# Two tiles' adapter rows in one turn, and 64-row products in pairs on the two halves of the array

## What is computed

```python
def _L1_cond_ref(x, adapter_mapping, W, b, lora_As, lora_Bs):
    base_out = jnp.einsum('bti,oi->bto', x, W) + b
    A = lora_As[adapter_mapping]
    Bm = lora_Bs[adapter_mapping]
    lora_h = jnp.einsum('bti,bir->btr', x, A)
    lora_out = jnp.einsum('btr,bro->bto', lora_h, Bm)
    return base_out + lora_out * SCALING
...
x = x + _L1_ffn_ref(_L1_cond_ref(x, itok_B_0_23, ...), ...)
```

## Time and profile before

| | |
|---|---|
| median of three runs | 466.69 us |
| the profiled execution | 466.59 us, span of its core 464.7 us |
| mean granted TensorE clock | 0.996 of full speed |
| TensorE matmuls | 2758, busy 447.0 us |
| VectorE, ScalarE, GpSimd busy | 306.9, 151.0, 72.6 us |
| a batch in the middle | about 38 us |

### The profile page before, as it was taken

How to read it: one execution, slowest core, us unless ns; L and a number is a source line. 1 busy time by engine, 2 the same in 40 slices (tenths; PEclk the granted TensorE clock), 3 DMA queues, 4 the chain that set the end, 5 groups by cost and what they waited for, 6 DMA issues and landing times.

```text
span 464.7 us, 7813 instructions
## 1 busy us (share of the span) xinstructions
PE 447.0 (96%) x2758; PEld 414.9 (89%) x2758; DVE 306.9 (66%) x911; ACT 151.0 (32%) x314; POOL 72.6 (16%) x62
## 2 busy tenths in 40 slices
PE   4988799999999999999999999999999999999997
PEld 4977799999988898889999999999999999999986
DVE  3897637574758688578557648738747755864852
ACT  4685212322222463234233224224323423321310
POOL 2040000000002412402402222120240230220110
PEclk9999899999999999999999999999999999999999
DMA  8993131111001101104103201211210310300302
GB/s 253 383 413 138 45 149 45 47 46 44 20 35 45 50 23 49 46 18 143 48 6 107 69 28 63 98 46 62 98 45 17 135 57 1 109 9 1 107 2 90
DMA packets 15151, 37.08 MB, mean 80 GB/s; under 512 B 2439, under 2 KB 7305, under 8 KB 15118
## 3 DMA queue, kind: packets, MB, share of 16 engines
q1 hardware_dynamic: 15022, 36.66, 22.7%
q0 software_dynamic: 96, 0.00, 0.2%
HBM read 27.07 MB, written 9.59 MB: 79 GB/s over the span
## 4 chain that ended last, share of the span: by engine, by line
PE 83%; DVE 12%; ACT 2%; issue 2%; DMA 1%; SPq 0%; DVEq 0%; ACTq 0%
PE banks L1239 25%; PE banks L1241 25%; PE banks L1240 25%; PE banks L1246 4%; DVE G L789 2%; DVE WbTlo L789 2%; PE banks L1471 2%; PE banks L1283 1%; DVE left L789 1%; DMA ws_lo_raw<-in_W_dram 1%; DVE ws_lo L789 1%; PE banks L1380 0%; DVE x_raw L973 0%; DVE G_raw L1086 0%; DVE w0s_lo L789 0%
## 5 line engine op out<-in xcount | busy, mean ns | idle before, releaser
L1239 PE MATMUL banks<-G,left 128*128 128x460 f32 x224 | 88.0, 393 | 0.0
L1240 PE MATMUL banks<-G,left 128*128 128x460 f32 x224 | 82.9, 370 | 0.0
L1241 PE MATMUL banks<-G,left 128*128 128x460 f32 x224 | 82.9, 370 | 0.0
L1239 PE MATMUL banks<-WbThi,ws_hi 128*128 128x460 f32 (+1 forms) x216 | 74.6, 345 | 4.3 <-DVE WbTlo L789 3.8
L474 POOL TENSOR_TENSOR xTlo<-x_raw,xThi 128x512 fp32r<-128x512 f32 x28 | 37.9, 1374 | 238.5 <-ACT xThi L572 114.6
L1241 PE MATMUL banks<-WbThi,ws_lo 128*128 128x460 f32 (+1 forms) x216 | 73.4, 340 | 0.0
L1240 PE MATMUL banks<-WbTlo,ws_hi 128*128 128x460 f32 (+1 forms) x216 | 73.1, 338 | 0.0
L526 ACT ACTIVATE left<-x_raw 128x512 fp32r<-128x512 f32 x64 | 38.7, 627 | 59.9 <-DVE x_raw L946 29.3
L1239 PEld LDWEIGHTS banks<-WbThi,ws_hi 128*128 128x128 f32 x216 | 40.6, 188 | 8.8 <-DVE WbTlo L789 4.9
L1239 PEld LDWEIGHTS banks<-G,left 128*128 128x128 f32 x224 | 42.4, 189 | 4.5 <-DVE wzTlo L789 0.3
L1241 PEld LDWEIGHTS banks<-G,left 128*128 128x128 f32 x224 | 42.1, 188 | 4.7
(11 more groups left out here) (178 smaller groups left out, 938.2 us busy)
## 6 DMA issues: line engine op xcount, KB each, us to landing
x_raw<-in_xT_dram SPq DMA_DIRECT2D x16, 512.0 KB, 3.8
out_dram<-ybuf SPq DMA_DIRECT2D x14, 512.0 KB, 2.7
x_raw<-in_W_dram SPq DMA_DIRECT2D x8, 512.0 KB, 3.3
WbTlo_raw<-in_F_dram SPq DMA_DIRECT2D x4, 920.0 KB, 12.8
w0s_lo_raw<-in_W_dram SPq DMA_DIRECT2D x6, 512.0 KB, 9.4
Fbuf<-fe_hi_dram SPq DMA_DIRECT2D x16, 64.0 KB
WbTlo_raw<-in_F_dram SPq DMA_DIRECT2D x1, 960.0 KB, 6.6
out_dram<-ybuf SPq DMA_DIRECT2D x3, 230.0 KB, 2.4
```

Of the source, the lines that this page charges most:

```text
L1239: pe.matmul(out_, l[0], r[0], start=start, stop=False, **kw)
L1240: pe.matmul(out_, l[0], r[1], start=False, stop=False, **kw)
L1241: return pe.matmul(out_, l[1], r[0], start=False, stop=stop, **kw)
```

## The change

`hs` becomes 128 columns wide: each tile gets one half of 64, with the three copies of h and the ones packed at 0, 17 and 34. One turn per batch (`turn_hs`, without arguments) transposes both, and one copy of ScalarE fills the one `hsT` of 128 rows, tile 0 in rows 0 to 63 and tile 1 in rows 64 to 127. `Ebuf` and `Fbuf` hold the slot's rows twice, once in each half, so SyncE issues six loads each instead of three. `adapter` and the new `adapters` issue one matmul of 64 rows for each tile, one right after the other, on the two halves; their results go to different PSUM banks. The F products leave `lora` and stand in pairs: the first two parts after `lora(0, 1)`, the third after `lora(1, 2)`. The turn and the E products take the places of the second tile's. The turn of `wz` of the first tile moves from step 22 to 24 in the batches that have a next one. `y_c12` waits for the last pair. The diff, cut to its core:

```diff
--- before.py
+++ after.py
+    HP = P // 2
...
-        Ebuf = sb("Ebuf", [96, RC], F32R)
+        Ebuf = sb("Ebuf", [P, RC], F32R)
...
-        hs = sb("hs", [P, 96], F32R)
+        hs = sb("hs", [P, P], F32R)
...
-        hsT = [sb(f"hsT{i}", [96, P], F32R) for i in range(2)]
+        hsT = sb("hsT", [P, P], F32R)
...
-        Fbuf = sb("Fbuf", [96, D], F32R)
+        Fbuf = sb("Fbuf", [P, D], F32R)
...
+        def hs_of(half):
+
+            return hs[:, half * HP:half * HP + 2 * (R + 1)], hs[:, half * HP + 2 * (R + 1):half * HP + 3 * R + 2]
+
+        def hs_rows(t, half):
+            return t[half * HP:(half + 1) * HP]
...
-            blocks = [(0, fe_hi_dram), (32, fe_lo_dram), (64, fe_hi_dram)]
+            blocks = [(half * HP + at, src) for half in range(2)
+                      for at, src in ((0, fe_hi_dram), (R + 1, fe_lo_dram), (2 * (R + 1), fe_hi_dram))]
+            bias_rows = [blocks[i] for i in (0, 1, 3, 4)]
 
             def load_e(b):
                 for p, src in blocks:
...
-            sp.wait_ge(memsets_done, 2)
+            sp.wait_ge(memsets_done, 1)
             load_e(0)
-            for p, src in blocks[0:2]:
+            for p, src in bias_rows:
                 sp.dma_start(Ebuf[p + R:p + R + 1, :].bitcast(F32), src[P:P + 1, 0:RC]).then_inc(e_in, 16)
...
-            sp.wait_ge(memsets_done, 3)
+            sp.wait_ge(memsets_done, 2)
             load_fb(0)
-            for p, src in blocks[0:2]:
+            for p, src in bias_rows:
                 sp.dma_start(Fbuf[p + R:p + R + 1, :].bitcast(F32), src[P:P + 1, RC:MC]).then_inc(f_in, 16)
...
-            def hsT_part(t, half):
-                wait_earlier(act, lora_done, t * 3 - 3 if not isinstance(t, int) or t > 1 else 0)
-                hi_half(ths_done, t + 1, hsT[half][:, :], pt_h1[0:96, :], hsT_ready)
+            def hsT_part(b):
+                wait_earlier(act, lora_done, b * 6)
+                hi_half(ths_done, b + 1, hsT[:, :], pt_h1, hsT_ready)
...
                 s_part(b, turn, 2)
-                hsT_part(m, 0)
-                hsT_part(m + 1, 1)
+                hsT_part(b)
...
-            dve.memset(hs[:, R:R + 1].bitcast(F32), 1.0).then_inc(memsets_done, 1)
-            dve.memset(hs[:, 32 + R:32 + R + 1].bitcast(F32), 1.0).then_inc(bias_step, 1)
+            for half in range(2):
+                for i in range(2):
+                    at = half * HP + i * (R + 1) + R
+                    ins = dve.memset(hs[:, at:at + 1].bitcast(F32), 1.0)
+            ins.then_inc(bias_step, 1)
...
             def y_c12(b):
                 dve.wait_ge(p_done, b * 7 + 7)
+                dve.wait_ge(lora_done, b * 6 + (6 if b < NB - 1 else 5))
...
             def hs_part(t, half):
 
                 dve.wait_ge(h1_done, t + 1)
-                wait_earlier(dve, ths_done, t)
-                dve.tensor_copy(hs[:, 0:64].rearrange("p (b c) -> p b c", b=2)[:, :, 0:R],
+                wait_earlier(dve, ths_done, t // 2)
+                twice, rest = hs_of(half)
+                dve.tensor_copy(twice.rearrange("p (b c) -> p b c", b=2)[:, :, 0:R],
                                 zd[half][:, 0:R].unsqueeze(1).broadcast_to([P, 2, R])).then_inc(hs_hi, 1)
                 dve.wait_ge(hs_hi, t + 1)
-                lo(hs[:, 64:64 + R], zd[half][:, 0:R], hs[:, 0:R]).then_inc(hs_ready, 1)
+                lo(rest, zd[half][:, 0:R], twice[:, 0:R]).then_inc(hs_ready, 1)
...
-                def lora(t, half, part):
-                    y0, w = Y_OF[part]
-                    y, s = ((dir_y(0), ca, cd), (dir_y(1), ce, cb))[half][part], slice(y0, y0 + w)
-                    three(y, (wzThi[:, :], wzTlo[:, :]), (B1Thi[:, s], B1Tlo[:, s]), False, False,
-                          skip_group_check=True)
-                    pe.matmul(y, hsT[half][:, :], Fbuf[:, s], start=False, stop=True, skip_group_check=True)\
-                      .then_inc(lora_done, 1)
-
-                def turn_hs(t):
-                    pe.wait_ge(hs_ready, t + 1)
-                    pe.transpose(pt_h1[0:96, :], hs[:, :].bitcast(F32), ident[:, :]).then_inc(ths_done, 1)
-
-                def adapter(t, half):
-                    pe.wait_ge(hsT_ready, t + 1)
-                    pe.wait_ge(e_in, b * 48 + 48 + 32)
-                    pe.matmul(zd[half][:, R:ZC], hsT[half][:, :], Ebuf[:, :], start=False, stop=True,
-                              skip_group_check=True).then_inc(z1_done, 1)
+                def y_of(half, part):
+                    return ((dir_y(0), ca, cd), (dir_y(1), ce, cb))[half][part]
+
+                def lora(half, part):
+                    s = slice(Y_OF[part][0], Y_OF[part][0] + Y_OF[part][1])
+                    return three(y_of(half, part), (wzThi[:, :], wzTlo[:, :]), (B1Thi[:, s], B1Tlo[:, s]), False, False,
+                                 skip_group_check=True)
+
+                def adapters(part):
+                    s = slice(Y_OF[part][0], Y_OF[part][0] + Y_OF[part][1])
+                    for half in range(2):
+                        ins = pe.matmul(y_of(half, part), hs_rows(hsT, half)[:, :], hs_rows(Fbuf, half)[:, s],
+                                        start=False, stop=True, skip_group_check=True)
+                    return ins
+
+                def turn_hs():
+                    pe.wait_ge(hs_ready, m + 2)
+                    pe.transpose(pt_h1, hs[:, :].bitcast(F32), ident[:, :]).then_inc(ths_done, 1)
+
+                def adapter():
+                    pe.wait_ge(hsT_ready, b + 1)
+                    pe.wait_ge(e_in, b * 96 + 96 + 64)
+                    for half in range(2):
+                        pe.matmul(zd[half][:, R:ZC], hs_rows(hsT, half)[:, :], hs_rows(Ebuf, half)[:, :],
+                                  start=False, stop=True, skip_group_check=True).then_inc(z1_done, 1)
...
                     add_lora0(a)
-                turn_hs(m)
                 main_to(19 + late)
-                adapter(m, 0)
-                turn_hs(m + 1)
+                turn_hs()
                 main_to(21 + late)
-                adapter(m + 1, 1)
+                adapter()
                 if has_a:
                     turn_small(wh_ready, a + 1, pt_wh, wh[:, :], twh_done)
...
                 main_to(22 + late)
                 if has_a:
                     small0(a + 1, main_tile, a * 2 + 2)
                     pe.wait_ge(whT_lo, a + 1)
-                main_to(26 if first else 22 if has_a else 24)
+                main_to(26 if first else 24)
                 turn_small(wz_ready, m + 1, pt_wz, wz[:, :], twz_done)
...
                 main_to(34)
-                pe.wait_ge(f_in, b * 48 + 48 + 32)
+                pe.wait_ge(f_in, b * 96 + 96 + 64)
                 if first:
                     pe.wait_ge(b1_lo, 1)
-                lora(m, 0, 0)
-                lora(m, 0, 1)
+                lora(0, 0)
+                lora(0, 1)
+                adapters(0).then_inc(lora_done, 1)
+                adapters(1).then_inc(lora_done, 1)
                 pe.wait_ge(c_kept, b * 3 + 2)
-                lora(m, 0, 2)
+                lora(0, 2).then_inc(lora_done, 1)
...
                         if g < 2:
-                            lora(m + 1, 1, g)
+                            lora(1, g).then_inc(lora_done, 1)
                 if not has_a:
-                    lora(m + 1, 1, 1)
+                    lora(1, 1).then_inc(lora_done, 1)
                 main_to(44 if has_a else 42)
                 pe.wait_ge(c_kept, b * 3 + 3)
-                lora(m + 1, 1, 2)
+                lora(1, 2)
+                adapters(2).then_inc(lora_done, 1)
                 if not has_a:
                     main_to(44)
-                    lora(m + 1, 1, 0)
+                    lora(1, 0).then_inc(lora_done, 1)
```

## The result

The changed kernel takes **471.75 us** (median of four runs, 471.54 to 473.81), beside 467.53 us for the kernel before in the same comparison (four runs): a ratio of 1.0108, 95% interval [1.0081, 1.0136]. Run again later it took 470.73 us beside 467.87, ratio 1.0067 [1.0047, 1.0086]. It is slower, by 0.7 to 1.1%, and both intervals are clear of 1. The forecast was 463.5 us, faster; the range held the time, the sign was wrong.

The account below looks back on a forecast made before the run. TensorE's issue was taken as the bound. Six middle batches saving 0.137 (place of h) plus 0.388 (F) give 3.15, plus 0.39 (batch 0), less 0.46 (batch 7): 3.08 off 466.59, so 463.5 us; range 462.2 to 473.0.

Parts of the forecast that it names:

- second load 0.013 late: E and F pairs: two loads need 0.22 us, the product before covers 0.207, so the second product starts 0.013 behind.
- the 0.05 allowed: Second quarter of `ffn0`: its cover product moves away, so up to 0.05 us a batch may be lost to the sum of x.
- the upper end: E and F pairs: loads of the two halves run side by side, saving 0.674 us a batch, or 462.4 us.
- late second loads: Rival at the pairs: each second load waits for the first product, 0.11 us between the two; 465.7 us, chance 0.16.
- no overlap: Rival at the pairs: the halves run one after the other, 0.2 us apart, F saves nothing; 467.0 us, chance 0.11.
- The turn alone: Place of h: one shared turn between 460-column products costs 0.113 us, as the turn of wz does.
- TensorE does not wait for `hg`: Middle batches: later wz work delays hg by 1.1 us at most; 0.36 us of cover is left, cost nothing.
- the new wait of `y_c12`: VectorE's last sum now waits for the last F pair: costs nothing, as the pair adds only 0.22 us.
- the 1.8 of the prediction: Batch 7, changed kernel: TensorE's wait for wz should be about 1.8 us of starts.
- its 0.7 for the kernel before: Batch 7, kernel before: TensorE's wait for wz taken as 0.7 us of starts.
- draining: First rival, at the pairs: array empties at each 128/64-row change, 0.166 us each, 48 changes, 8.0 us; 471.5 us, chance 0.33.
- The remark that loads never overlap: Weight loads: the prediction said the loads of this trace never overlap, but all fill the same rows; no size given.

Follow-up runs that it names:

- the 128-row kernel: Changed kernel with two copies of the turned h, the other tile's half zero, so every product of h takes 128 rows: 466.34 us, ratio 0.9973.
- the kernel on one half: Changed kernel with both products of each pair on the first half of the rows: 475.56 us, ratio 1.0173.
- two copies: Changed kernel with ScalarE's copy of the turned h in two pieces of 64 rows, products untouched: 470.03 us, ratio 1.0061.
- the split pairs: Changed kernel with the first F pair right behind its own part's three matmuls, four 64-row places a batch instead of three: 473.24 us, ratio 1.0116.

## Why the prediction was wrong

**The step that failed** is the price of a pair: "second load 0.013 late" and then pure streaming, as if a 64-row product stood in the stream like any other. Entering and leaving a place was put at nothing; the runs showed 0.28 to 0.38 us a place more than forecast. By place, in a middle batch:

| place | forecast us | measured us |
|---|---|---|
| the shared turn | 0.113 | 0.113 (334.11 to 334.43, less 0.207) |
| E pair and turn of `wh` | 0.196 | 0.526 |
| first two F pairs | 0.440 | 0.716 (348.42 to 349.55, less 0.414) |
| last F pair | 0.220 | 0.598 |

The three places with 64 rows are 0.98 us dearer than forecast. A middle batch became 0.50 longer where 0.525 less was forecast, a miss of 1.025. The second quarter of `ffn0` took 0.10 more than without its cover (354.18 to 354.57 is 0.39; before, 0.11 to the F product there, 0.11 to `ffn0` and 0.18 to its next, so 0.29 were left), twice the 0.05 allowed. VectorE's sum of x, for which TensorE waits there, and the weight loads show why:

```profile
353.60 0.69 DVE L958 TENSOR_TENSOR x_raw<-banks,x_raw 128x512 f32<-128x512 f32 x1 [1.09 <-PE banks L1255]
```
```profile
354.13 0.19 PEld L1255 LDWEIGHTS banks<-ws_hi,wzTlo 128*128 128x128 f32 x1
354.34 0.19 PEld L1253 LDWEIGHTS banks<-whThi,BwThi 128*128 128x128 f32 x1
```

The sum ends at 354.29, and the load for `ffn0` comes at 354.34, 0.21 behind the one before it in place of 0.11. So the sum is late, and this part belongs to the order and not to the borders: the 128-row kernel has the same stretch of 0.38 (349.38 to 349.76), its sum ending at 349.47. Some 0.06 the other way I cannot place.

**What held.** The halves are independent; their loads even run side by side, two in 0.19 us, which was the upper end. Both other rivals, late second loads (0.11 apart) and no overlap, are refuted by the pair's common start and by the kernel on one half. The turn alone is exact. TensorE does not wait for `hg` in a middle batch, and the new wait of `y_c12` shows nowhere. In batch 7 the turn of `wz` comes 1.00 us later, counted from the batch's first product with `G` (444.49 - 438.34 before, 451.32 - 444.17 now), where 0.85 was forecast; the E pair starts 0.09 later than forecast and its record is 0.10 longer, and that makes the other 0.15. TensorE's idle wait went from 0.58 to 1.43; in starts it was 0.95 and is 1.79, so the 1.8 of the prediction is right and its 0.7 for the kernel before was misread.

**The rival that came true** is the first, draining, at a chance of 0.33; its 471.5 us lies beside the 471.75 measured, but that nearness is partly luck: it forecast 4.9 us more than before, the batches lost 4.2, and its terms were not quite these. It took 0.166 a change for emptying, or 0.276 if the next load must wait too. By the estimate above the emptying is 0.09 and the load does wait, 0.11: about 0.2 a border, of which a middle batch shows 0.98/6 = 0.16 net against the forecast. The Trainium skill, TensorEngine Tiling (Array Packing), Key Properties, says that changing the tiling mode drains TensorE and that different tiles load and multiply in parallel. The traces bear out both sentences; I had weighed the first against the fact that products of 96 rows and 128 stand side by side at no cost, and that was no evidence on 64: products of 96 rows pay no border, products of 64 pay two, alone or in pairs. The remark that loads never overlap was a misreading too: in rows 4 records of 0.19 us start 0.11 apart.

**The sum.** In the batches the forecast was 3.08 us saved, the traces show 4.2 lost, a miss of 7.3: 6 x 1.025 = 6.15 in the middle batches, 0.54 in batch 0 (0.15 lost, 0.39 saved forecast), and 0.60 in batch 7 (1.06 lost, 0.46 forecast). In batch 7 the turn of `wz` is 0.15 later than forecast and the F places behind it cost about 0.8 more; about 0.35 the other way falls in front of the batch's products with `G`, where a wait of 0.24 for VectorE (at 432.59 before) is gone. The last 0.9 of the 8.2 us between 463.5 and 471.75 comes from the base: the sum started from an execution of 466.59, and the comparison's median before is 467.53. Of the 4.2 us lost the places with 64 rows make 3.56 (294.11 with two copies, less 290.55). The remaining 0.6 is less than the 1.1 that the collision of the last section costs the changed kernel, and the kernel before has a like one.

## What to carry to other kernels

A change of the array between whole and half costs some 0.2 us each way here, by the estimate above as two things that were free before: the next weight load under the running product, and the tail of that product. With 0.39 of overhead a place and 0.207 saved by each pair of 460 columns, two such pairs in one place would break even (an estimate, not tried). The runs say: fewer places (the split pairs cost 0.26 us a batch more), or leave such products on 128 rows with zeros. Before pricing an instruction by its neighbours, ask whether it changes a setting of the engine that all the neighbours share, and give that its own price.

## What the runs showed of the hardware that was not expected

An addition of 128x8 elements on VectorE takes 0.17 us, but in batch 7 it took 1.25 in the kernel before. GpSimd's and VectorE's timelines of that trace:

```profile
442.80 1.29 POOL L474 TENSOR_TENSOR left<-x_raw,left 128x512 fp32r<-128x512 f32 x1 [2.26 <-ACT left L526]
```
```profile
442.86 1.25 DVE L894 TENSOR_TENSOR gf<-gaf,gbf 128x8 f32<-128x8 f32 x1
```

The same two of the changed kernel:

```profile
449.66 1.26 POOL L484 TENSOR_TENSOR left<-x_raw,left 128x512 fp32r<-128x512 f32 x1 [2.97 <-ACT left L536]
```
```profile
449.71 1.23 DVE L906 TENSOR_TENSOR gf<-gaf,gbf 128x8 f32<-128x8 f32 x1
```

And with two copies:

```profile
447.96 1.28 POOL L484 TENSOR_TENSOR left<-x_raw,left 128x512 fp32r<-128x512 f32 x1 [3.11 <-ACT left L536]
```
```profile
447.88 0.17 DVE L909 TENSOR_TENSOR gf<-gaf,gbf 128x8 f32<-128x8 f32 x1
```

Where GpSimd has started first, by 0.05 to 0.06 us, VectorE's addition ends only with GpSimd's instruction (442.86 + 1.25 = 444.11, 442.80 + 1.29 = 444.09), and the whole stop stands in its record as duration, not as idle time. Where VectorE is first, by 0.08 to 0.09, both run at their own pace. All 13 traces fall into one of the two: eight have the long addition, five the short. The price is 1.06 us of VectorE, and 1.1 us of the changed kernel's batches (295.21 less 294.11). What it costs the kernel before was not tried. The Trainium skill, SBUF — State Buffer, SBUF: two separate sides, has the rule (a VectorE operation with two inputs in SBUF and one of GpSimd exclude each other, and the first keeps the ports for its whole instruction); these traces agree. Why ScalarE's copy, which releases GpSimd, starts 0.14 us later behind the E pair with two small copies than with one (447.26 - 445.65 and 448.96 - 447.49) was not tried.

The kernel before has a second such case in the same batch, just ahead of the first:

```profile
439.25 1.30 POOL L474 TENSOR_TENSOR left<-x_raw,left 128x512 fp32r<-128x512 f32 x1 [22.56 <-ACT left L526]
```
```profile
439.67 1.42 DVE L973 TENSOR_TENSOR x_raw<-x_raw 128x512 f32<-128x512 f32 x1
```

In the other batches this subtraction of VectorE takes 0.68 us. It is why VectorE took up the gates of batch 7 only at 441.01, though the E product they need, at 440.33, was done by 440.56. In the changed kernel VectorE's instruction comes first and takes 0.68 (444.86), and it is GpSimd's, begun at 445.08, that is longer: 1.61.
